# One core, eight stages: two PSUM banks shared by turns in the local layers, and the MLP norm's mean and variance in column quarters

## The chip, the cores and the metric

The program runs on 1 core of one Trainium2 chip. The time is the device time of one execution in microseconds, the median of three runs. The trace is of one further execution, taken by the hardware profiler. PE is TensorE, PEld its weight loads, DVE is VectorE, ACT is ScalarE, POOL is GpSimd, SP is SyncE, which here only issues DMAs.

## The reference

A stack of eight stages works on x of 16 sequences x 256 tokens x 128 channels, all in float32. The first seven (a random-feature attention, a router feed-forward, a cosine attention, an int4 linear layer, a state-space layer, an expert feed-forward, a gated recurrence) are touched only at the start and in the state-space layer. The last one, the local transformer, holds half the time:

```python
def attn_layer(x, Wqkv, qs, ksc, Wo):
    q, k, v = ...                      # 16 heads of 64
    q = l2norm(q) * qs ; k = l2norm(k) * ksc
    q = q * cos * scale + rotate_half(q) * sin * scale
    k = k * cos * inv + rotate_half(k) * sin * inv
    return local_attention(q, k, v) @ Wo        # window of 32
def ffn_layer(x, g, bln, W1, b1, W2, b2):
    mu = x.mean(-1, keepdims=True)
    var = ((x - mu) ** 2).mean(-1, keepdims=True)
    xn = (x - mu) / jnp.sqrt(var + 1e-05) * g + bln
    a, gate = jnp.split(xn @ W1 + b1, 2, -1)
    return a * jax.nn.gelu(gate, approximate=False) @ W2 + b2
for i in range(6):
    x = attn_layer(shift_tokens(x), ...) + x
    x = ffn_layer(shift_tokens(x), ...) + x
x = x + that_stack(_layernorm(x))
```

The state-space layer runs h = exp(delta A) h + delta x B over 256 tokens for 256 channels and 16 states, with an output projection.

## The kernel before

It is one program without a planner. Each stage is a block in which every engine has its own instruction stream, written out as a loop over steps; the streams are tied by semaphores, and each engine runs its stream in order. So the order of the work is the order of the calls in each engine's loop.

**Local layers** (`local_layers`). Tokens stand in 8 groups of 512 (two sequences), channels on the partitions (tile `y`). A step i takes one group and one quad of heads (four heads): 4 steps are a group, 32 a layer, N = 192 steps make the 6 layers. Work on different steps overlaps: step i projects queries and keys of quad i, norms those of i-1, scores i-2, takes values of i-2 and i-3. In this text a step has two halves:

- first half on PE: `project(4i)` (L2254, one 128x512 matmul), `project_v(2i)` (L2267), `norm(i-1)` (L2274), `score` of the even sequence (L2289), `project(4i+1)`, `values` of an odd sequence (L2309 for the values, L2313 for the sums that give the denominators);
- second half: `project(4i+2)`, `project_v(2i+1)`, `score` of the odd sequence, `project(4i+3)`, `values` of an even sequence.

The MLP of a group and the output projection lie between these calls, at fixed places by step modulo 4 (`mlp_at(i, k)`). I call the steps by what they carry: i mod 4 = 2 is the **out step** (L2324, output projection in two parts, the third gate matmul and gelu), 3 the **widen step** (three L2341), 0 the **back step** (L2363 in the first half; `center_mlp` L2332 and `variance` L2337 in the second), 1 the **gate step** (`make_gate` 0 and 1, L2341, in the second half; POOL's `scale_mlp` L2657 and ACT's `make_z` L2470 before them).

PSUM has 8 banks. All four projections of queries and keys go through bank 0, so `project(c)` waits for `squared` of c-1: DVE has multiplied the bank by the rotary tables (`rotate_start`, L2539 and L2540), and ACT has squared it (`square`, L2433). Bank 1 carries the values' projection, copied out by ACT (`copy_v`, L2449), and by turns the denominators, read by ACT (`take_den`, L2425 and L2427). Banks 2 to 5 are scores, 6 the values, and bank 7 (`X_BANK`) everything else: the norm's sums, output projection, mean, variance, gates, MLP; `take_x` makes each user wait until the one before has been read out.

The chain of a step's norm: `square` on ACT, `sum_squares` on POOL (L2645), `norm` on PE in the next step, `clamp` on DVE, `invert_norm` on ACT, four DMAs by SP that spread 32 rows to 128 (`send_inverse`), and `unite` on POOL (L2653), then the scores.

ACT's order in a first half: copy_v, square(4i), invert_norm, exp (L2455), square(4i+1), take_den, make_z. In a second: copy_v, square(4i+2), exp, take_gate (L2477), square(4i+3), take_den.

The MLP norm: PE multiplies `y` by the 128x128 matrix I - 1/128 (`center`), DVE copies the result to SBUF (L2577), ACT squares it, PE multiplies it by a 128x128 matrix of ones, so the variance stands on all 128 rows, and ACT takes Ln and Exp of 128x512.

**Prologue of the local layers**: DVE takes the statistics of all 32 tiles, and the 8 groups are normalized, transposed and copied one after another before the first step. **Start of the program**: SP issues the DMAs of x, nine constants and the weights of six stages, and only then do the engines begin. **State-space layer** (`state_space`): 16 steps (states) for each of 8 groups; the next group's statistics and transposes (MEASURE, NORMALIZE, TURN, TURNED) lie in steps 0 to 3, where the former group's gating, output projection (step 3, 12 small matmuls in one go) and addition (step 4) lie too.

## Time and profile before

| | |
|---|---|
| median of 3 runs | 6519.71 us (6516.19 to 6521.88) |
| profiled execution | 6522.74 us, span 6520.8 us |
| local layers, from first to last record | 3201.5 to 6518.1 us |
| granted TensorE clock, mean | 0.947 |

PE is busy for 90% of the span by its records, DVE for 67%, ACT 52%, POOL 35%. A record of a matmul is longer than the time in which the next one can start, so this text measures PE by the distance of the starts of neighbouring groups, not by their lengths. In the timeline a row is a group of equal neighbours: start, length, engine, line, operation, operands, count, and in brackets the idle time ahead of it and what ended it.

### The profile page before, as it was taken

To read this page: it belongs to the slowest core of one execution; us is meant where nothing else is said; L and a number is where in the kernel's file an instruction comes from. 1 tells how busy PE (TensorE), PEld (TensorE's weight loads), DVE (VectorE), ACT (ScalarE), POOL (GpSimd) and SP (SyncE) were. 2 spreads that over 40 slices of the span, in tenths; PEclk is the share of its full clock that TensorE was granted. 3 is DMA by queue.
4 is the path that set the end of the run, shared out by engine and by line. 5 is a ranking of instruction groups with operands and counts; after the bars stand their busy time and mean duration, and the time that the engine had idled before them with its cause. 6 is when DMAs were issued, how large, how long until landed. Compare 5 with 4: busy or idle time off the path is not lost.

```text
span 6520.8 us, 129965 instructions
## 1 busy us (share of the span) xinstructions
PE 5878.9 (90%) x51681; PEld 3219.8 (49%) x51681; DVE 4384.8 (67%) x7178; ACT 3402.6 (52%) x5560; POOL 2289.2 (35%) x1597
## 2 busy tenths in 40 slices
PE   7999878999677778998689999999999999999998
PEld 3555554444422225765445555555555555555554
DVE  4656434454288894334678888888878788887885
ACT  3444324656144443444456656666666666665664
POOL 0111101222034441000055555555555555555553
PEclk9999978999688888998799999999999999999998
DMA  5555302333100000000011111111111111111110
GB/s 138 115 115 119 89 0 53 80 82 83 44 3 0 0 0 1 1 0 1 24 36 32 40 43 34 31 47 37 34 45 38 33 44 40 34 39 41 38 37 24
DMA packets 298945, 275.95 MB, mean 42 GB/s; under 512 B 40580, under 2 KB 289572, under 8 KB 298148
## 3 DMA queue, kind: packets, MB, share of 16 engines
q1 hardware_dynamic: 298372, 268.00, 17.7%
q8 instruction: 397, 6.50, 0.4%
q14 instruction: 176, 1.44, 0.1%
HBM read 30.88 MB, written 2.10 MB: 5 GB/s over the span
## 4 chain that ended last, share of the span: by engine, by line
PE 33%; issue 5%; DVE 5%; POOL 5%; ACT 2%; DMA 0%; POOLq 0%; DVEq 0%; SPq 0%; ACTq 0%
PE banks L2254 7%; PE banks L2289 6%; PE banks L2324 5%; PE banks L2309 4%; PE banks L2267 3%; PE banks L2341 3%; DVE local_probs L2559 2%; POOL local_rot L2653 2%; POOL local_ssum L2645 2%; PE banks L2363 2%; PE banks L2313 2%; PE banks L2274 1%; ACT local_probs L2455 1%; DVE local_gate L2584 1%; DVE local_sin L2540 1%
## 5 line engine op out<-in xcount | busy, mean ns | idle before, releaser
L2645 POOL TENSOR_TENSOR local_ssum<-local_sq 128x512 f32<-128x512 f32 x384 | 697.5, 1816 | 2145.1 <-ACT local_sq L2433 2144.6
L2653 POOL TENSOR_TENSOR local_rot<-local_rot,local_inv_all 128x512 f32<-128x512 f32 x768 | 964.6, 1288 | 94.1 <-DMA local_inv_all<-local_inv 93.6
L2254 PE MATMUL banks<-local_y,local_Wqkv 128*128 128x512 f32 x1536 | 823.0, 618 | 64.0 <-ACT local_sq L2433 61.2
L2559 DVE TENSOR_TENSOR local_probs<-banks,band 128x576 f32<-128x576 f32 x768 | 546.2, 753 | 185.4 <-PE banks L2289 180.1
L2455 ACT ACTIVATE local_probs<-local_probs,local_npeak 128x1152 f32<-128x1152 f32 x384 | 482.8, 1257 | 357.1 <-DVE local_probs L2559 357.1
L2539 DVE TENSOR_TENSOR local_rot<-banks,local_rotary_scaled 128x512 f32<-128x512 f32 x768 | 525.6, 684 | 191.1 <-PE banks L2254 185.6
L2433 ACT ACTIVATE local_sq<-banks 128x512 f32<-128x512 f32 x768 | 459.4, 598 | 253.6 <-DVE local_sin L2540 244.8
L2546 DVE TENSOR_TENSOR local_rot<-local_rot,local_sin 128x1024 f32<-128x1024 f32 x384 | 513.7, 1338 | 41.9 <-DVE local_sin L2540 2.3
L2449 ACT COPY local_v<-banks 128x512 f32<-128x512 f32 x384 | 224.9, 586 | 594.1 <-PE banks L2267 593.6
L2289 PEld LDWEIGHTS banks<-local_rot 32*128 32x128 f32 x12288 | 416.7, 186 | 225.0 <-issue 200.8
L2540 DVE TENSOR_TENSOR local_sin<-banks,local_rotary_scaled 128x512 f32<-128x512 f32 x768 | 522.4, 680 | 0.0
L2309 PEld LDWEIGHTS banks<-local_probs,local_v 128*32 128x32 f32 x12288 | 345.4, 110 | 301.8 <-issue 291.9
L2289 PE MATMUL banks<-local_rot 32*128 32x160 f32 (+1 forms) x12288 | 490.2, 296 | 0.0
L1361 POOL TENSOR_TENSOR mamba_seen<-mamba_state,mamba_c_wide 128x1024 f32<-128x1024 f32 x128 | 301.0, 2352 | 474.2 <-DVE mamba_state L1442 474.2
L2309 PE MATMUL banks<-local_probs,local_v 128*32 128x160 f32 (+1 forms) x12288 | 458.5, 290 | 0.5 <-DVE local_oT L2567 0.5
L2254 PEld LDWEIGHTS banks<-local_y,local_Wqkv 128*128 128x128 f32 x1536 | 264.3, 190 | 372.1 <-ACT local_sq L2433 249.5
L1031 POOL TENSOR_TENSOR cosine_summed<-cosine_probs 128x512 f32<-128x512 f32 x128 | 162.4, 1269 | 696.1 <-ACT cosine_probs L919 696.1
L2267 PE MATMUL banks<-local_Wqkv,local_y 128*128 128x512 f32 x768 | 396.0, 597 | 0.0
L2324 PE MATMUL banks<-local_oT,local_Wo 128*128 128x512 f32 x768 | 354.9, 605 | 0.9 <-ACT local_gate L2477 0.9
L1258 PE MATMUL banks<-mamba_seen,ident 128*128 128x512 f32 x512 | 289.2, 693 | 64.8 <-DVE mamba_xs L1449 42.3
L2341 PE MATMUL banks<-local_mlp_z,local_W 128*128 128x512 f32 (+1 forms) x576 | 328.2, 652 | 11.9 <-DVE local_gate L2584 4.2
L487 POOL TENSOR_TENSOR favor_summed<-favor_probs 128x256 f32<-128x256 f32 x128 | 93.0, 727 | 689.3 <-DVE favor_probs L443 689.3
(400 smaller groups left out, 10561.4 us busy)
## 6 DMA issues: line engine op xcount, KB each, us to landing
local_inv_all<-local_inv SPq DMA_DIRECT2D x768, 128.0 KB, 2.7
favor_half_norm_all<-favor_half_norm SPq DMA_DIRECT2D x512, 128.0 KB, 3.0
cosine_inv_all<-cosine_inv SPq DMA_DIRECT2D x256, 128.0 KB, 2.6
favor_rden<-favor_inv SPq DMA_DIRECT2D x256, 64.0 KB, 2.1
cosine_rden<-cosine_inv_den SPq DMA_DIRECT2D x256, 64.0 KB, 2.1
local_Wqkv<-in_L_ffn_Wqkv_quads SPq DMA_DIRECT2D x36, 256.0 KB, 2.9
local_Wo<-in_L_ffn_Wo_quads SPq DMA_DIRECT2D x6, 512.0 KB, 4.1
experts_w_W<-in_L_ffn_W SPq DMA_DIRECT2D x1, 2048.0 KB
```

The costliest lines, as they stand in the source:

```text
L2254: pe.matmul(seqs(banks[:, QK_BANK, :]), Wqkv[:, at:at + P], y_group(g), start=True, stop=True).then_inc(qk_projected, 1)
L2267: pe.matmul(banks[:, V_BANK, :], y[:, 2 * g + tile // ST, at:at + P], Wqkv[:, V_COLUMNS(half)], start=True, stop=True).then_inc(v_projecte ...
L2289: last = pe.matmul(banks[:, S_BANK + r, lo:hi], k[rows_r, half, at:at + P], q[rows_r, half, at:at + hi - lo], start=(half == 0), stop=(hal ...
L2309: last = pe.matmul(banks[rows_r, O_BANK, part * SEQ + at:part * SEQ + to], v[:, G % 2, s * ST + tile, c:c + 32], probs[:, e % 3, r, lo:hi] ...
L2324: last = pe.matmul(banks[:, X_BANK, :], Wo[:, j, :], oT[:, (QUADS * G + j // 2) % (QUADS + 1), j % 2, :], start=(j == 0), stop=(j == 2 * Q ...
L2341: pe.matmul(banks[0:m, X_BANK, :], W1[:, column + lo:column + lo + m], z[:], start=True, stop=True).then_inc(signal, 1)
L2455: act.activation(a, a, ACT.Exp, bias=npeak[:, layer:layer + 1], scale=SCALE).then_inc(exped, 1)
L2539: dve.tensor_tensor(seqs(rot[:, k % ROTATED, half, :]), raw, twice(table[:, m, 0, half, :]), ALU.mult).then_inc(cosined, 1)
L2540: dve.tensor_tensor(seqs(sin[:, m, half, :]), raw, twice(table[:, m, 1, half, :]), ALU.mult).then_inc(sined, 1)
L2559: dve.tensor_tensor(probs[:, e % 3, r:r + 2, :], banks[:, S_BANK + r:S_BANK + r + 2, 0:SCORES], consts["band"].unsqueeze(1).broadcast_to([ ...
L2645: pool.tensor_tensor(ssum[:, n % 2, m, :], sq[:, 0, :], sq[:, 1, :], ALU.add).then_inc(square_summed, 1)
L2653: pool.tensor_tensor(a, a, twice(inv_all[:, n % 2, m, of_seq(s)]), ALU.mult).then_inc(united, 1)
```

## The change

It replaces several things at once.

1. **Local layers, banks.** Bank 0 now carries the even halves of queries and keys and the denominators, bank 1 the odd halves and the values' projection. `values` makes the denominators first, in bank 0, with a signal of its own (`den_summed`); ACT's `take_den` is cut in two, `log_den` (reads the bank) ahead of `exp` in ACT's order, and `invert_den` where take_den stood.
2. **Local layers, MLP norm.** The mean is four 128x32 by 128x128 matmuls (`mean`, in the widen step), read by ACT into `token_stat` (128x128), spread by four DMAs to 128x512; POOL subtracts (`center_mlp`, last in its step). The variance is made the same way, in the second half of the back step ahead of `project(4i+3)`; ACT's `root` works on 128x128 and stands ahead of `square(4i+3)`; four DMAs spread it; `scale_mlp` on POOL now stands behind `sum_squares(2i)`. DVE's copy goes.
3. **Local layers, prologue.** Only group 0 is prepared ahead; groups 1 to 7 in steps 0 to 7. The rotary tables of a layer are scaled in two parts around the layer's first step.
4. **State-space layer.** MEASURE to TURNED move to steps 12 to 15 of the former group, the output projection is cut in halves over steps 3 and 4, the addition goes to step 5.
5. **Start.** Only four constants, the first stage's weights and x are issued ahead; the other 43 DMAs go into SP's stream of the first stage, in its steps 1 to 6.

```diff
@@ start
-                for n in consts:
+                for n in FAVOR_CONSTS:
...
-                for name in ("router", "cosine", "int4", "mamba", "hgrn"):
-                    ws[name].load(sp)
@@ favor_attention, sync
+                    if i == LOADS:
+                        for tile, source in w["later_consts"]:
+                            sp.dma_start(tile, source).then_inc(w["consts_loaded"][0], 16)
+                    if 0 < i - LOADS <= len(w["later"]):
+                        w["later"][i - LOADS - 1].load(sp)
@@ state_space
-        0, 1, 2, 3, 5, 7, 8, 9, 10, 11, 12, 13, 14
-    GATE, WAY_OUT, ADD_OUT = 2, 3, 4
+        -4, -3, -2, -1, 5, 7, 8, 9, 10, 11, 12, 13, 14
+    GATE, WAY_OUT, ADD_OUT = 2, (3, 4), 5
@@ local_layers
-    QK_BANK, V_BANK, S_BANK, O_BANK, X_BANK = 0, 1, 2, 6, 7
+    DEN_BANK, V_BANK, S_BANK, O_BANK, X_BANK = 0, 1, 2, 6, 7
+    qk_bank = lambda c: (DEN_BANK, V_BANK)[c % 2]
@@ tensor, project
-                    if c:
-                        pe.wait_ge(squared, c)
+                    if half:
+                        pe.wait_ge(v_copied, c // 2 + 1)
+                    elif n >= 3:
+                        pe.wait_ge(den_logged, 2 * n - 5 + m)
+                    elif c:
+                        pe.wait_ge(squared, c - 1)
@@ project_v
-                    if j >= 6:
-                        pe.wait_ge(den_logged, j - 5)
-                    elif j:
-                        pe.wait_ge(v_copied, j)
+                    if j:
+                        pe.wait_ge(squared, 2 * j)
@@ values
+                    at_step = n + 2 + s
                     pe.wait_ge(exped, e + 1)
+                    if at_step < N:
+                        pe.wait_ge(squared, 4 * at_step + 3 - 2 * s)
+                    elif e:
+                        pe.wait_ge(den_logged, e)
+                    for lo, hi, tile in ((0, BAND, 0), (BAND, SCORES, 1)):
+                        for r in range(4):
+                            at = tile * P
+                            last = pe.matmul(banks[32 * r:32 * r + 32, DEN_BANK, at:at + hi - lo], consts["ones"][:, 0:32],
+                                             probs[:, e % 3, r, lo:hi], start=(tile == 0), stop=(tile == 1), skip_group_check=True)
+                    last.then_inc(den_summed, 1)
@@ mean, variance
-                    pe.matmul(seqs(banks[:, X_BANK, :]), center[:], y_group(G % GROUPS), start=True, stop=True).then_inc(centering, 1)
+                    for c in range(GT):
+                        at = c % ST * P
+                        last = pe.matmul(banks[32 * c:32 * c + 32, X_BANK, 0:P], consts["ones"][:, 0:32],
+                                         y[:, 2 * (G % GROUPS) + c // ST, at:at + P], start=True, stop=True)
...
-                    pe.matmul(banks[:, X_BANK, :], consts["ones"], msq[:], start=True, stop=True).then_inc(var_summed, 1)
+                    for c in range(GT):
+                        last = pe.matmul(banks[32 * c:32 * c + 32, X_BANK, 0:P], consts["ones"][:, 0:32], msq[:, c * P:(c + 1) * P],
+                                         start=True, stop=True)
@@ tensor, the order
+                    if (G := mlp_at(i, 7)) is not None:
+                        mean(G)
                     if i < N:
                         project(4 * i + 1)
...
                     if (G := mlp_at(i, 8)) is not None:
-                        center_mlp(G)
+                        variance(G)
...
-                    if (G := mlp_at(i, 8)) is not None:
-                        variance(G)
@@ scalar, the order
                         invert_norm(i - 1)
+                    if (e := within(2 * (i - 3) + 1)) is not None:
+                        log_den(e)
                     if (e := within(2 * (i - 2))) is not None:
                         exp(e)
+                    if (G := mlp_at(i, 7)) is not None:
+                        take_mean(G)
+                    if (G := mlp_at(i, 8)) is not None:
+                        square_mlp(G)
                     if i < N:
                         square(4 * i + 1)
                     if (e := within(2 * (i - 3) + 1)) is not None:
-                        take_den(e)
+                        invert_den(e)
...
+                    if (e := within(2 * (i - 2))) is not None:
+                        log_den(e)
                     if (e := within(2 * (i - 2) + 1)) is not None:
                         exp(e)
...
                     if (G := mlp_at(i, 8)) is not None:
-                        square_mlp(G)
+                        root(G)
                     if (G := mlp_at(i, 9)) is not None:
                         take_gate(G, 0)
                     if i < N:
                         square(4 * i + 3)
                     if (e := within(2 * (i - 2))) is not None:
-                        take_den(e)
-                    if (G := mlp_at(i, 8)) is not None:
-                        root(G)
+                        invert_den(e)
@@ gpsimd, the order
+                    if i < N:
+                        sum_squares(2 * i)
                     if (G := mlp_at(i, 9)) is not None:
                         scale_mlp(G)
-                    if i < N:
-                        sum_squares(2 * i)
...
                         sum_squares(2 * i + 1)
+                    if (G := mlp_at(i, 7)) is not None:
+                        center_mlp(G)
@@ sync
+                def send_token_stat(into, sent):
+                    for c in range(GT):
+                        rows_c = token_stat[32 * c:32 * c + 32, :]
+                        source = bass.AP(rows_c.tensor, rows_c.offset, [rows_c.ap[0], [0, 4], rows_c.ap[-1]])
+                        sp.dma_start(into[:, c * P:(c + 1) * P], source).then_inc(sent, 16)
```

## Rows read from the trace of the kernel before

**Rows 1.** The page, busy time of each engine
```profile
PE 5878.9 (90%) x51681; PEld 3219.8 (49%) x51681; DVE 4384.8 (67%) x7178; ACT 3402.6 (52%) x5560; POOL 2289.2 (35%) x1597
```

**Rows 2.** Timeline, first output-projection matmuls of two neighbouring groups
```profile
5006.01 3.70 PE L2324 MATMUL banks<-local_oT,local_Wo 128*128 128x512 f32 x8
...
5071.77 3.70 PE L2324 MATMUL banks<-local_oT,local_Wo 128*128 128x512 f32 x8
```

**Rows 3.** Timeline of PE in one gate step, and the next step's start
```profile
5052.61 0.67 PE L2313 MATMUL banks<-local_probs,ones 128*32 128x160 f32 x16
5053.99 1.12 PE L2254 MATMUL banks<-local_y,local_Wqkv 128*128 128x512 f32 x2 [0.71 <-ACT local_sq L2433]
5054.95 1.02 PE L2267 MATMUL banks<-local_Wqkv,local_y 128*128 128x512 f32 x2
5055.90 1.27 PE L2289 MATMUL banks<-local_rot 32*128 32x160 f32 x32
...
5058.06 1.02 PE L2254 MATMUL banks<-local_y,local_Wqkv 128*128 128x512 f32 x2
5059.02 1.19 PE L2309 MATMUL banks<-local_probs,local_v 128*32 128x160 f32 x32
5060.02 0.67 PE L2313 MATMUL banks<-local_probs,ones 128*32 128x160 f32 x16
5060.62 1.13 PE L2341 MATMUL banks<-local_mlp_z,local_W 128*128 128x512 f32 x2
...
5062.44 1.02 PE L2267 MATMUL banks<-local_Wqkv,local_y 128*128 128x512 f32 x2
5063.40 0.64 PE L2274 MATMUL banks<-local_ssum,local_heads 128*32 128x256 f32 x8
```

**Rows 4.** Timeline of ACT in that step
```profile
5054.66 0.80 ACT L2470 ACTIVATE local_mlp_z<-local_mlp_yc,local_ln_b,local_ln_g 128x512 f32<-128x512 f32 x1
...
5058.70 1.26 ACT L2455 ACTIVATE local_probs<-local_probs,local_npeak 128x1152 f32<-128x1152 f32 x1 [1.40 <-DVE local_probs L2559]
5059.86 0.67 ACT L2477 ACTIVATE local_gate<-banks,local_b 128x512 f32<-128x512 f32 x1
5060.45 0.60 ACT L2433 ACTIVATE local_sq<-banks 128x512 f32<-128x512 f32 x1
5060.94 0.38 ACT L2425 ACTIVATE local_rden<-banks 128x256 f32<-128x256 f32 x1
```

**Rows 5.** Timeline of POOL: that step's sum of squares, a later scaling of the MLP
```profile
5061.12 1.80 POOL L2645 TENSOR_TENSOR local_ssum<-local_sq 128x512 f32<-128x512 f32 x1 [0.41 <-ACT local_sq L2433]
...
5114.36 1.27 POOL L2657 TENSOR_TENSOR local_mlp_yc<-local_mlp_yc,local_mlp_sq 128x512 f32<-128x512 f32 x1 [0.30 <-ACT local_mlp_sq L2465]
```

**Rows 6.** Timeline of PE in a back step: the centering matmul and its follower
```profile
5108.24 1.13 PE L2332 MATMUL banks<-local_y,local_center 128*128 128x512 f32 x2
5109.20 1.02 PE L2254 MATMUL banks<-local_y,local_Wqkv 128*128 128x512 f32 x2
```

**Rows 7.** Busy time by stretches: us, each engine (instructions), granted clock, DMA share, GB/s
```profile
3236.00:3290.00 54.00, 38.21 (x209) 15.24 (x210) 31.69 (x51) 17.07 (x30) 20.84 (x14) 0.73 0.09 20
3290.00:3350.00 60.00, 52.94 (x694) 29.37 (x693) 47.58 (x66) 31.56 (x52) 35.24 (x24) 1.00 0.16 37
```

**Rows 8.** Timeline of the start: issue of x's rest, its use by DVE
```profile
9.12 1.14 SPq L2860 DMA_DIRECT2D x<-in_L_attn_x  x1
...
41.27 0.86 DVE L402 BATCH_NORM_STATS2 favor_stats<-x 128x6 f32<-128x128 f32 x4
```

**Rows 9.** DMA view of 0 to 80 us: KB each, median us to landing
```profile
x<-in_L_attn_x SPq DMA_DIRECT2D x1, 0.5 KB, 13.3
```

**Rows 10.** Timeline of the state-space layer: DVE behind the output projection
```profile
2090.88 1.23 DVE L1432 TENSOR_TENSOR banks<-mamba_dx,banks 128x1024 f32<-128x1024 f32 x1 [2.68 <-PE banks L1247]
```

**Rows 11.** Timeline of the local prologue: SP's last load, first table scaling
```profile
3213.79 0.37 SPq L2160 DMA_DIRECT2D local_W<-in_L_ffn_W  x1
...
3236.59 0.35 DVE L2527 TENSOR_SCALAR local_rotary_scaled<-local_rotary,local_qk_scales 128x256 f32<-128x256 f32 x1 [0.32 <-PEq L2168]
```

More of the change, by code:

```diff
@@ L1274, in _ @@
                         gather(k - 2)
-                    if (g := finish_at(k, WAY_OUT)) is not None:
-                        project_out(g)
+                    for half in range(2):
+                        if (g := finish_at(k, WAY_OUT[half])) is not None:
+                            project_out(g, half)
                     if (m := make_at(k, TURN)) is not None:
@@ L2216, in _ @@
                 act.preload_act_table_set(EXP_LN)
-                act.wait_ge(var_done, 1)
-                act.activation(ln_log, ln_var, ACT.Ln).then_inc(log_done, 1)
-                act.wait_ge(log_done, 1)
-                act.activation(ln_rstd, ln_log, ACT.Exp, scale=-0.5).then_inc(rstd_ready, 1)
-                for g in range(GROUPS):
-                    act.wait_ge(turned, g + 1)
-                    act.copy(y[low, 2 * g:2 * g + 2, 0:SEQ], seqs(banks[low, g, :])).then_inc(y_low, 1)
+                root_x(act, 0)
+                copy_x(act, 0)
             @block.tensor
             def _(pe):
-                for g in range(GROUPS):
-                    pe.wait_ge(normed, (g + 1) * GT)
-                    for tile in range(GT):
-                        last = pe.transpose(banks[:, g, tile * P:(tile + 1) * P], xn[:, g * GT + tile, :], consts["ident"])
-                    last.then_inc(turned, 1)
+                turn_x(pe, 0)
         with nc.Block() as block:
@@ L2432, in square @@
                         act.wait_ge(square_summed, c // 2)
[L2433 removed]
+                    act.activation(sq[:, c % 2, :], banks[:, qk_bank(c), :], ACT.Square).then_inc(squared, 1)
                 def invert_norm(n):
```

208 lines of the change are left out of this document (137 added, 71 removed).

## Prediction

> **What bounds the kernel now.** I read the page first: PE is busy for 90% of the span, DVE for 67% [rows 1]. Half of the time is the local layers, so I took a period of them, one group in four steps: from one output projection to the next 65.76 us [rows 2]. Then the timeline of PE through the four steps, reading only starts. In the gate step one group of matmuls follows the other at a fixed distance (for instance 0.96, 0.95, 0.96, 1.00, 0.60) but for one place: the sums of L2313 start at 5052.61, and the next projection not 0.60 but 1.38 us behind them, and the bracket names ACT's square as releaser [rows 3]. That 0.78 us is the only stall that I find in the period, so PE has 65.0 us of work in 65.8. DVE, in a stretch of the same loop, is busy for 48 of 60 us where PE has 53 [rows 7]. So the local layers are bound by PE. PE's stream is in order: what is taken from its work is gained, and a wait that is put into it counts in full, since nothing later can be pulled ahead of it.
>
> **PE's work.** The centering matmul takes 0.96 us to its follower [rows 6], and the variance has the same shape. Each becomes four 128x32 matmuls over 128 columns. The nearest rows are the norm's four over 256 columns, 0.64, and the eight of the denominators, 0.60 for 1152 columns [rows 3]; half of the first is 0.32, 512 of 1152 columns of the second are 0.27. I take 0.35 (bounds 0.25 and 0.64). So 1.92 becomes 0.70: a gain of 1.22 us per group. The denominators only change places with the values. The 0.78 us of today's wait goes too, and what is late next is counted now.
>
> **The waits.** I count from T, the start of a half step's odd projection (`project(4i+1)` or `project(4i+3)`). By today's distances, PE's stream behind it, with nothing of the MLP between, is: denominators at 1.05 (1.00 for the projection by its rows, up to 0.05 more where no MLP matmul stood ahead), the rest of `values` to 2.65, the even projection (5060.62 to 5062.44, less 0.96 for the gate matmul) to 3.5, the values' projection (0.96) to 4.46, where in the second half the norm follows [rows 3].
> On ACT `log_den` now stands ahead of `exp`. It waits for the denominators: 1.05 + 0.67 [rows 3] + 0.07 for the signal (from square's end to POOL's start in rows 4 and 5) = T+1.79, and takes 0.38 [rows 4]. So `exp` starts at T+2.20, where today it starts as soon as the mask is done, and frees ACT 1.16 later [rows 4]: T+3.36. `square` takes 0.60 [rows 4]: T+3.96. POOL's sum takes 1.75 to 1.80 [rows 5], so the norm can start at T+5.85. Since the odd projection now sits in bank 1, the values' projection waits for that same square: T+4.02. Put against PE's stream:
> - gate step, first half: the values' projection wants T+3.50, gets T+4.02: 0.52 us.
> - gate step, then: `scale_mlp` now stands behind `sum_squares(2i)` on POOL: 3.96 + 0.07 + 1.76 + 1.27 [rows 5] = 7.06, `make_z` 0.80 [rows 4], signals: 7.95. PE wants the first gate matmul at 4.02 + 0.95 + 1.20 (scores: 5055.90 to 5058.06 less the gate matmul) = 6.17. Wait 1.8 us. Today `make_z` is done at 5055.46, before the scores have even begun [rows 3, 4].
> - gate step, second half: the second gate matmul needs bank 7 emptied by `take_gate` (0.67, rows 4), which is behind `exp`: T+4.08, wanted at T+2.65: 1.43 us. The norm is then no longer late.
> - widen step, first half: the same with `take_mean` (128x128; between half and the whole of the 0.38 in rows 4, I take 0.28): the first L2341 gets T+3.69, wants T+2.65: 1.04 us.
> - widen step, second half: one L2341 lies between, the norm wants T+5.41, gets T+5.85: 0.44 us.
> - back step, second half: the variance that filled 0.96 us here has moved ahead, and `root` (Ln and Exp of 128x128, 0.45 to 0.9, I take 0.66) stands between `exp` and `square`. Square ends at T+4.62. The values' projection waits 1.16, and the norm, at T+6.50, another 0.88: 2.04 us.
> - out step: the output projection and the third gate matmul cover all of it: 0.
> The spreads of mean and variance are covered: POOL uses the mean at the end of that step, the variance a step later; SP's four issues each stand behind those of `send_inverse`, and nobody waits for what comes behind them. POOL's new subtraction (bounds 1.27 and 1.80, rows 5) is last in its step, ahead of a wait for the next squares.
> Sum of waits 7.27 us. The period becomes 65.76 - 0.78 - 1.22 + 7.27 = 71.03, +5.27. DVE loses a copy and stays below PE. For 46 of the 48 groups (the first and the last are not in the pattern): +242 us. Bounds: with the 0.4 and 0.5 terms gone and half of the gate step's, +3 a group, +140; with 0.2 us more at each of seven waits, +6.7, +308.
>
> **The rest.** Start: DVE gets to the second group at 41.27, long after x's rest has landed at 9.12 + 13.3 = 22.4 us [rows 8, 9]. With five constants fewer ahead and nothing behind, it lands at 18 to 20 (estimate), so the start gains 21 to 23. Against it 43 DMAs of 0.4 to 1.1 us of issue [rows 8, 11], some 25 us of SP's time, go between the first stage's own transfers, where SP has gaps: I charge 5 (0 to 20). Net -17 (-24 to 0). State-space layer: DVE waits 2.68 us per group behind the output projection [rows 10]; halving it gains at most that, for 8 groups -20 (-30 to 0; it would cost if the statistics, now in steps 12 to 15, delayed DVE there). Local prologue: the tables are scaled from 3236.6, and SP's loads end at 3214.2 [rows 11], which now becomes the limit: -22, of which the preparation of groups 1 to 7 in the early steps gives some 7 back: -15 (-22 to -3). Scaling the tables, eight of at most 0.35 us [rows 11] at each layer's start, now lies largely beside PE's work: -7 (-11 to 0). Together -59 (-87 to -3).
>
> Sum: +242 - 59 = +183 on the profiled execution of 6522.7, so 6706; the median lies 3 us lower: **6703**.
>
> **The rivals.**
> Waits that vanish (other side). If PE had slack that I overlook, or `exp` did not have to wait for `log_den`, only the work counts: 65.76 - 0.78 - 1.22, -2.0 a group, -96, and -59: 6365 us. For it speaks that two banks now share eight fillings by turns, where one had four that each waited for DVE and ACT. Against it: this wait is 0.78 us of 65.8 today, and the places of the calls fix mine. It decides from where the waits sum to under 3.3 us per group. Chance 0.12.
> Waits of half my size, 3.7 us, if they overlap with each other more than I count: about 6535. Chance 0.11 (0.04 of it faster, 0.05 the same, 0.02 slower).
> A lower clock. In 3236 to 3290, with PE busy for 38 of 54 us, the granted clock was 0.73; in the next stretch, 53 of 60 us, it was 1.00 [rows 7], the higher of its two levels (2.4 GHz). With my waits PE is busy for about 90% of a period, so I expect 1.00. Should 4 us of matmuls in each group run at 1.2 GHz, they take 4 us more, +190: 6890. Chance 0.08. The Trainium skill (TensorE: Matmul & The Clock Gate, section A second HAM failure mode: psum-queue depth-cycling) says that a kernel that cycles through PSUM banks can idle so often for moments that the clock swings between its levels; by that rule this rival would be the likely one. The stretch with 53 of 60 us speaks against it.
> That the change doesn't do what it says: the early loads may slow the first stage by all that the start gains. It costs 20 us and is in the range.
>
> **How the numbers follow.** My forecast has 0.69, the others 0.12, 0.11, 0.08. Faster by over 0.2% (13 us, about what a measurement of this kernel tells from no change): 0.12 + 0.04 = 0.16. Same 0.05. Slower 0.69 + 0.08 + 0.02 = 0.79. The range: the low bounds, +140 - 87 = +53, are widened to the half-sized waits: 6510; the high ones, +308 - 3 = +305, give 6825, of which I take 6810, since not all come together. Outside lie the vanished waits, the fast part of the half-sized ones and half of the lower clock, 0.2.
>
> **What would show it.** In the local layers of the changed kernel: 71 us between output projections; 1.8 us of idle PE ahead of the first gate matmul with `make_z` as releaser, 1.4 ahead of the second with ACT's gate copy; 1.0 ahead of the first widening matmul with `take_mean`; 2 us in two parts ahead of the norm behind the back step; ACT's `exp` starting 2.2 us behind the odd projection in every half. The clock stays 1.00. The state-space layer is 20 us shorter and the first stage ends 17 us earlier. If the period is under 65.8 us, my reading of ACT's order is wrong.

## The result, and the profile after

The changed kernel takes 6596.2 us (median of four runs, 6595.5 to 6598.6) where the kernel before takes 6518.0 on the same chip (6512.9 to 6521.9): ratio 1.0119, interval 1.0104 to 1.0134. It is 78 us slower; the forecast was 183 us slower, 6703 us. The sign and the places of the waits were right, the size was not. The profiled executions lie 74.3 us apart (spans 6520.8 and 6595.1).

From the page of the changed kernel, busy time of each engine [against rows 1]:

```profile
PE 5843.6 (89%) x52257; PEld 3191.9 (48%) x52257; DVE 4346.5 (66%) x7129; ACT 3319.8 (50%) x5630; POOL 2137.8 (32%) x1645
```

PE has 35 us less to do, and the span is 74 us longer: the time is in PE's waits. By the first and last record of each layer the 74 us split so: the first layer ends 18.8 us earlier, the state-space layer is 8.9 us shorter (696.3 to 687.5), the local layers need 18.3 us less from their first record to their first output projection (138.1 to 119.8), and 117.9 us more from the first to the 48th (3120.7 to 3238.6). The rest adds 2.4 us, in pieces of under 2.

Two neighbouring output projections in the timeline of PE [against rows 2]:

```profile
5024.49 3.70 PE L2358 MATMUL banks<-local_oT,local_Wo 128*128 128x512 f32 x8
...
5093.75 3.70 PE L2358 MATMUL banks<-local_oT,local_Wo 128*128 128x512 f32 x8
```

The period is 69.26 us, and nearly all 47 are within 0.05 of it. In the kernel before they were not alike: 65.75 to 66.1 in most periods of the middle layers, up to 67.4 in the others, 68 to 70.7 at the five boundaries between layers. Without the last period, which is cut short in both, the mean is 66.63 before and 69.22 after.

The gate step of the changed kernel on PE, with idle time and releaser in brackets [against rows 3]. L2285 projects, L2334 is the denominators, L2346 the values, L2296 the values' projection, L2318 the scores, L2382 the gate matmuls:

```profile
5001.15 1.12 PE L2285 MATMUL banks<-local_y,local_Wqkv 128*128 128x512 f32 x2
5002.20 0.70 PE L2334 MATMUL banks<-local_probs,ones 128*32 128x160 f32 x16
5002.72 1.16 PE L2346 MATMUL banks<-local_probs,local_v 128*32 128x160 f32 x32
5003.81 1.12 PE L2285 MATMUL banks<-local_y,local_Wqkv 128*128 128x512 f32 x2
5005.03 1.12 PE L2296 MATMUL banks<-local_Wqkv,local_y 128*128 128x512 f32 x2
5006.09 1.27 PE L2318 MATMUL banks<-local_rot 32*128 32x160 f32 x32
5008.54 1.10 PE L2382 MATMUL banks<-local_mlp_z,local_W 128*128 128x512 f32 x2 [1.18 <-issue]
5009.47 1.02 PE L2285 MATMUL banks<-local_y,local_Wqkv 128*128 128x512 f32 x2
...
5013.35 1.13 PE L2382 MATMUL banks<-local_mlp_z,local_W 128*128 128x512 f32 x2 [1.24 <-ACT local_gate L2530]
```

ACT and POOL in the same stretch [against rows 4, 5]. L2469 is `log_den`, L2501 `exp`, L2479 `square`, L2523 `make_z`, L2530 `take_gate`, L2711 the sum of squares, L2727 `scale_mlp`:

```profile
5002.97 0.38 ACT L2469 ACTIVATE local_rden<-banks 128x256 f32<-128x256 f32 x1 [1.15 <-PE banks L2334]
5003.25 1.25 ACT L2501 ACTIVATE local_probs<-local_probs,local_npeak 128x1152 f32<-128x1152 f32 x1
5004.40 0.59 ACT L2479 ACTIVATE local_sq<-banks 128x512 f32<-128x512 f32 x1
...
5007.63 0.81 ACT L2523 ACTIVATE local_mlp_z<-local_mlp_yc,local_ln_b,local_ln_g 128x512 f32<-128x512 f32 x1 [2.25 <-POOL local_mlp_yc L2727]
...
5011.47 1.25 ACT L2501 ACTIVATE local_probs<-local_probs,local_npeak 128x1152 f32<-128x1152 f32 x1
5012.62 0.68 ACT L2530 ACTIVATE local_gate<-banks,local_b 128x512 f32<-128x512 f32 x1
```

```profile
5005.06 1.30 POOL L2711 TENSOR_TENSOR local_ssum<-local_sq 128x512 f32<-128x512 f32 x1 [5.73 <-ACT local_sq L2479]
5006.32 1.27 POOL L2727 TENSOR_TENSOR local_mlp_yc<-local_mlp_yc,local_mlp_sq 128x512 f32<-128x512 f32 x1
```

The chain for the first gate matmul is read downwards: square to 5004.99, sum to 5006.36, scaling to 5007.59, `make_z` to 5008.44, matmul at 5008.54. The bracket of that matmul names no releaser ("issue"); in 39 of 45 groups the list below names `make_z`. The second stands behind `log_den`, `exp` and `take_gate`. The other waits of a group that have a bracket, in the widen and the back step (L2507 is `take_mean`, L2644 is `hide`, DVE's step of the MLP that multiplies the widened part by its gate):

```profile
5041.63 1.12 PE L2382 MATMUL banks<-local_mlp_z,local_W 128*128 128x512 f32 x2 [0.83 <-ACT local_token_stat L2507]
...
5052.27 0.64 PE L2303 MATMUL banks<-local_ssum,local_heads 128*32 128x256 f32 x8 [0.34 <-DVE local_gate L2644]
...
5067.23 1.13 PE L2296 MATMUL banks<-local_Wqkv,local_y 128*128 128x512 f32 x2 [0.69 <-ACT local_sq L2479]
5068.59 0.64 PE L2303 MATMUL banks<-local_ssum,local_heads 128*32 128x256 f32 x8 [0.23 <-POOL local_ssum L2711]
```

The view that should have been read first is the list of PE's waits over all the local layers, 3300 to 6400 us (what waited, for whom: us in total, times, longest). Before:

```profile
PE banks L2254 <- ACT local_sq L2433: 45.1, 58, 2.1
PE banks L2274 <- DVE local_gate L2584: 17.2, 28, 0.9
PE banks L2274 <- POOL local_ssum L2645: 13.1, 20, 1.9
```

After:

```profile
PE banks L2382 <- ACT local_gate L2530: 56.0, 45, 1.2
PE banks L2382 <- ACT local_mlp_z L2523: 47.6, 39, 1.2
PE banks L2382 <- ACT local_token_stat L2507: 36.7, 44, 0.8
PE banks L2296 <- ACT local_sq L2479: 32.7, 47, 0.8
PE banks L2303 <- DVE local_gate L2644: 15.8, 44, 0.7
PE banks L2303 <- POOL local_ssum L2711: 10.8, 46, 1.0
PE banks L2382 <- issue: 7.1, 6, 1.2
```

In sum 75 us of waits before, 207 after. Before there were three kinds of them, not one: besides the 0.71 to 0.78 in every group, PE waited in some groups for DVE's `hide(G, 2)` and for POOL's sum ahead of the norm.

### The profile page after: what moved, and what is told of

Read it like the earlier page. It is cut to its first block and busy times, and to the rows that moved or that the text cites. A ratio compares the mean times of both kernels' runs of the same rounds, so it can differ in the third digit from the quotient of the medians.

```text
span 6595.1 us, 132318 instructions
## 1 busy us (share of the span) xinstructions
PE 5843.6 (89%) x52257; PEld 3191.9 (48%) x52257; DVE 4346.5 (66%) x7129; ACT 3319.8 (50%) x5630; POOL 2137.8 (32%) x1645
## 5 line engine op out<-in xcount | busy, mean ns | idle before, releaser
L2711 POOL TENSOR_TENSOR local_ssum<-local_sq 128x512 f32<-128x512 f32 x384 | 498.9, 1299 | 2445.0 <-ACT local_sq L2479 2437.7
L2719 POOL TENSOR_TENSOR local_rot<-local_rot,local_inv_all 128x512 f32<-128x512 f32 x768 | 958.9, 1282 | 61.6 <-DMA local_inv_all<-local_inv 61.1
L2285 PE MATMUL banks<-local_y,local_Wqkv 128*128 128x512 f32 x1536 | 821.8, 617 | 12.3 <-PEq L2215 8.0
L2479 ACT ACTIVATE local_sq<-banks 128x512 f32<-128x512 f32 x768 | 455.8, 594 | 158.8 <-DVE local_sin L2603 156.9
L2609 DVE TENSOR_TENSOR local_rot<-local_rot,local_sin 128x1024 f32<-128x1024 f32 x384 | 498.3, 1298 | 41.9 <-DVE local_sin L2603 2.3
L2318 PEld LDWEIGHTS banks<-local_rot 32*128 32x128 f32 x12288 | 416.4, 186 | 225.0 <-issue 208.2
L2318 PE MATMUL banks<-local_rot 32*128 32x160 f32 (+1 forms) x12288 | 489.7, 296 | 0.5 <-POOL local_rot L2719 0.5
L2501 ACT ACTIVATE local_probs<-local_probs,local_npeak 128x1152 f32<-128x1152 f32 x384 | 478.6, 1246 | 3.7 <-DVE local_probs L2622 3.6
L2382 PE MATMUL banks<-local_mlp_z,local_W 128*128 128x512 f32 (+1 forms) x576 | 328.1, 652 | 168.0 <-ACT local_gate L2530 59.9
L2346 PE MATMUL banks<-local_probs,local_v 128*32 128x160 f32 (+1 forms) x12288 | 448.0, 286 | 0.3 <-DVE local_oT L2631 0.3
L2296 PE MATMUL banks<-local_Wqkv,local_y 128*128 128x512 f32 x768 | 403.5, 607 | 44.4 <-ACT local_sq L2479 39.9
L2469 ACT ACTIVATE local_rden<-banks 128x256 f32<-128x256 f32 x384 | 147.6, 384 | 585.9 <-PE banks L2334 585.6
L2631 DVE TENSOR_TENSOR local_oT<-banks,local_rden 128x512 f32<-128x512 f32 x384 | 265.3, 691 | 221.6 <-ACT local_rden L2473 213.0
L2285 PEld LDWEIGHTS banks<-local_y,local_Wqkv 128*128 128x128 f32 x1536 | 263.6, 189 | 276.4 <-issue 227.5
L2346 PEld LDWEIGHTS banks<-local_probs,local_v 128*32 128x32 f32 x12288 | 376.5, 110 | 9.5 <-issue 0.5
```

The source lines that it names most:

```text
L2285: pe.matmul(seqs(banks[:, qk_bank(c), :]), Wqkv[:, at:at + P], y_group(g), start=True, stop=True).then_inc(qk_projected, 1)
L2296: pe.matmul(banks[:, V_BANK, :], y[:, 2 * g + tile // ST, at:at + P], Wqkv[:, V_COLUMNS(half)], start=True, stop=True).then_inc(v_projecte ...
L2318: last = pe.matmul(banks[:, S_BANK + r, lo:hi], k[rows_r, half, at:at + P], q[rows_r, half, at:at + hi - lo], start=(half == 0), stop=(hal ...
L2346: last = pe.matmul(banks[rows_r, O_BANK, part * SEQ + at:part * SEQ + to], v[:, G % 2, s * ST + tile, c:c + 32], probs[:, e % 3, r, lo:hi] ...
L2479: act.activation(sq[:, c % 2, :], banks[:, qk_bank(c), :], ACT.Square).then_inc(squared, 1)
L2501: act.activation(a, a, ACT.Exp, bias=npeak[:, layer:layer + 1], scale=SCALE).then_inc(exped, 1)
```

## The experiments

The theory: what is slow is the order of the steps on ACT and POOL. `log_den` waits for the denominators until T+1.8 (T: start of the odd projection of a half step) and holds `exp` back; the small steps that empty bank 7 (`take_mean`, `root`, `take_gate`) stand behind both; `scale_mlp` stands behind the sum of squares. The main rival: the two shared banks, or the MLP norm by transfers, cost the time themselves, and a wait taken away comes back at the next shared bank. "A mean period" below leaves out the cut last one of 47; it is 66.63 before and 69.22 changed. Times are medians of four to eleven executions, but for three runs with one (named there). The cuts of code show the calls alone, without the conditions around them.

**Order, one engine at a time.** POOL alone (e1):

```diff
-                    if i < N: sum_squares(2 * i)
                     if (G := mlp_at(i, 9)) is not None: scale_mlp(G)
+                    if i < N: sum_squares(2 * i)
```

> POOL only: scale_mlp goes back ahead of sum_squares(2i), as in the kernel before. Theory (order of steps on ACT and POOL makes the waits): make_z then ends at about T+5 of the gate step, the first gate matmul's wait of 1.25 us goes, the other waits stay (0.36, 1.32, 0.91, 0.41, 0.96, 0.41). 1.25 x 46 = 57: 6539 us, period 67.97. Rival (the two shared banks or the transfers themselves cost the time, and a wait that is taken away comes back at the next shared bank): the wait moves to the gate step's second half, 6585 to 6600 us.

Measured 6536.7 us, mean period 68.03 (-1.19). The 47.6 us of waits for `make_z` are gone; 56.0 for the gate copy, 37.5 for `take_mean` and 33.4 for the square stand as they were, within 1 us. The wait did not come back.

ACT alone, the small steps (e2):

```diff
-    log_den(2(i-3)+1); exp(2(i-2)); take_mean(G)
+    take_mean(G); log_den(2(i-3)+1); exp(2(i-2))
...
-    log_den(2(i-2)); exp(2(i-2)+1); root(G); take_gate(G, 0)
+    root(G); take_gate(G, 0); log_den(2(i-2)); exp(2(i-2)+1)
```

> ACT only: take_mean, root and take_gate(G, 0), the three that empty bank 7, go ahead of log_den, which waits for the denominators until T+1.8 anyway. Theory: the second gate matmul's wait of 1.32 and the first widening matmul's 0.91 go, the values' projection of the back step waits 0.36 instead of 0.96: 2.83 x 46 = 130: 6466 us, period 66.4. Rival (shared banks): ACT's exp and square do not move, so PE is held one step later by the square, and no more than 1 us a group is gained: 6550 or more.

Measured 6475.4 us, mean period 66.76 (-2.46): the theory's terms (2.83) within a sixth, and 75 us below the rival's bound.

ACT alone, the two long ones (e3):

```diff
-    log_den(2(i-3)+1); exp(2(i-2))
+    exp(2(i-2)); log_den(2(i-3)+1)
...
-    log_den(2(i-2)); exp(2(i-2)+1)
+    exp(2(i-2)+1); log_den(2(i-2))
```

> ACT only: exp goes ahead of log_den in both halves, as in the kernel before; the small steps stay behind both. Theory: in the second halves of gate and back step the mask is long done and exp starts 1.5 to 2.7 us earlier, so gate1's wait falls from 1.32 to 0.2 and the back step's 0.96 and 0.41 vanish; in the first halves exp starts only 0.5 earlier, log_den ends at T+3.1, and the even projection of the gate step, which now needs the denominators' bank, waits 0.45 that it did not wait: together -2.65 a group, 6474 us. Rival (log_den must stand first because the banks are shared): the even projections of all four steps wait 0.5 each: -0.5 a group, 6570.

Measured 6478.6 us, mean period 66.79 (-2.43). PE's waits in the local layers, two of them:

```profile
PE banks L2285 <- ACT local_rden L2469: 18.9, 43, 0.5
PE banks L2382 <- ACT local_token_stat L2507: 11.5, 46, 0.3
```

The first is new: the even projection now waits for `log_den`, once a group, 0.44 us, since the denominators share its bank. This is all that `log_den` ahead of `exp` protects: 0.44 us in one half step of eight, where `log_den` behind `exp` gains 2.9 in the others.

POOL's order and ACT's small steps together (e4, the edits of e1 and e2):

> The edits of e1 and e2 together. Theory: the terms add, since they lie at different places of the group: 1.25 + 2.83 = 4.08 us, 188 in all: 6408 us, period 65.1, faster than the kernel before. Rival: they overlap, because the shorter gate step leaves the mask and exp later against the odd projection: 6440 or more.

Measured 6439.6 us, mean period 66.10: 1.2% faster than the kernel before (ratio 0.9878, 0.9861 to 0.9894), but 32 us short of the sum of the terms, which is the rival's number (6440 or more). The rival put it down to a later `exp`; the list of waits names POOL and, with 18.7 us, `hide(G, 2)`, and POOL's timeline shows it (L2719 is `unite`, four in a row):

```profile
PE banks L2303 <- POOL local_ssum L2711: 36.7, 76, 1.9
```

```profile
5059.94 5.96 POOL L2719 TENSOR_TENSOR local_rot<-local_rot,local_inv_all 128x512 f32<-128x512 f32 x4 [0.92 <-DMA local_inv_all<-local_inv]
5065.86 1.27 POOL L2711 TENSOR_TENSOR local_ssum<-local_sq 128x512 f32<-128x512 f32 x1
```

In the gate step the second sum of squares stands behind four unites, which start only when the transfer of the inverse norms has landed. With a shorter gate step PE gets to the norm before POOL gets to the sum.

**Exp where its mask is ready.** In the second halves of the back and the gate step `exp` went ahead of `log_den` as well (e5: `root`, `take_gate`, `exp`, `log_den`):

> The edits of e4, and in the second halves of the back and the gate step exp goes ahead of log_den too (behind root or take_gate), since the mask is done there before log_den's wait ends. Theory: the back step's square ends at T+3.4 instead of 3.84, so its two waits (0.36 for the values' projection, 0.36 for the norm, 0.04 and 0.29 beyond the bare distance) shrink by 0.5 to 0.7, and the gate step's norm wait (0.44 idle, POOL's unites start late) by 0.1 to 0.4, since that norm chain starts earlier: -0.6 to -1.1 a group, 6390 to 6410 us. Rival (POOL's chain of unites is what binds now): only the back step's 0.3 goes, 6425.

Measured 6425.0 us, mean period 65.59: the rival's number. What PE still waited for was POOL's sum, 29.4 us, and DVE's `hide(G, 2)`, 18.3 us.

**POOL's and DVE's order too (e10).**

```diff
-    unite x4; sum_squares(2 * i + 1)
+    unite x2 (first sequence); sum_squares(2 * i + 1); unite x2 (second)
...
-    normalize(2(i-2)); hide(G, 2)
+    hide(G, 2); normalize(2(i-2))
```

> The edits of e5, and two more changes of order: on POOL sum_squares(2i+1) goes between the unites of the two sequences (the second pair is needed a half step later), on DVE hide(G, 2) goes ahead of normalize, which waits for invert_den. Theory: the gate step's norm no longer waits for POOL's four unites (mean 0.41 a group beyond the bare 0.95), the widen step's norm no longer for hide(G, 2) (0.41 to 0.55): -0.8 a group, 6387 us, period 64.5. Rival (the scores of the next step then wait for the later unites, or DVE's normalize comes late): the gain is under 0.3 a group, 6411 or more.

Measured 6382.7 us (6381.6 to 6386.7), ratio 0.9796 (0.9781 to 0.9811): 2.0% faster than the kernel before, 3.2% faster than the changed one. Nearly every period away from a boundary is 64.48 or 64.49; in e5 they ran from 64.9 to 66.5. PE's two longest waits in the local layers are

```profile
PE banks L2303 <- POOL local_ssum L2714: 11.0, 48, 1.5
PE banks L2382 <- DVE local_gate L2647: 5.4, 5, 2.5
```

**Which part of the change costs.** The changed kernel with the old MLP norm (e6), and the kernel before with the new one (e7); each change of code is the hunks for `center_mlp`, `mean`, `variance`, `take_mean`, `root`, `take_centered`, `scale_mlp`, `send_mean` and `send_rstd`, backward or forward.

> The changed kernel with the MLP norm of the kernel before (centering matmul, DVE copy, full-width variance behind the values, root behind the denominators, scale_mlp ahead of the sum of squares); the two shared banks stay. Theory, against 6596: +1.20 us of PE work a group; waits -1.25 (scale), -0.91 (take_mean), -0.85 (variance covers the back step's norm again); the gate copy's 1.32 stays: -1.8 a group, 6512 us, period 67.1. Rival A (the shared banks are the cost): 6590 or more. Rival B (the banks are free, the new norm is the whole cost): period at 65.0 to 65.7, 6430 to 6460.

> The kernel before with the new MLP norm alone (mean and variance on 32 rows by quarters, spread by transfers, in the places of the change); one bank for the projections and ACT's order of exp ahead of the denominators stay. Theory, against 6516: PE work -1.20 a group; new waits 0.85 (scale behind the sum), 0.45 (mean's copy behind exp), 1.05 (root ahead of square in the back step, where the variance no longer covers it): +1.15, 6570 us. Rival (the norm is a pure gain, the two banks make the waits): -1.20 a group, 6460.

Measured 6561.4 and 6547.4 us, mean periods 68.57 and 67.26: +1.94 and +0.63 against 66.63, together +2.57, where the whole change has +2.59. (e6 also holds the change's new places of the tables and of the prologue.) So the parts add up, and neither of the rivals "the one is free" holds: as placed, the banks cost three times what the norm does. Both forecasts were off, by 49 us upward and 23 downward. With the banks alone PE waits

```profile
PE banks L2371 <- ACT local_mlp_sq L2498: 57.4, 45, 1.3
PE banks L2375 <- ACT local_gate L2516: 56.0, 45, 1.2
```

The first line I had not foreseen: with the old norm `square_mlp` too stands behind `log_den` and `exp`, and the variance matmul waits 1.28 us for it. It is the same mechanism once more. With the norm alone

```profile
PE banks L2254 <- ACT local_sq L2440: 86.5, 146, 3.1
PE banks L2348 <- ACT local_mlp_z L2484: 31.7, 39, 0.8
```

the scaling behind the sum costs 0.81 to 0.88 a group as counted (0.85), `root` ahead of the square 0.60 instead of my 1.05, and the mean's copy 0.05 instead of 0.45. A fourth wait was not in my sum: in the back step the odd projection stands 0.73 us behind the variance that now takes 0.36, since the square is not done, which is 0.37 more (the 146 waits of the first line are three a group). With it the terms give 0.65 a group (1.85 of waits less 1.20 of work), and 0.63 was measured.

**The kernel before, with orders alone.** POOL's order (e13), then POOL's, DVE's and ACT's (e14):

> The kernel before with POOL's order of e10 alone: sum_squares(2i+1) between the unites of the two sequences. Theory (the periods of the kernel before lie between 65.75 and 67.1 because that sum stands behind four unites and their transfer): PE's 13.1 us of waits for POOL's sum go, and the periods away from a layer's boundary become equal: -13 us, 6503. Rival (the spread of the periods has another source, or the sum is then still late): 6510 to 6516.

Measured 6504.3 us (ratio 0.9978, 0.9969 to 0.9987), the theory's number. Nearly every period away from a boundary is 65.75 now, so it was POOL's order that spread them. The boundary periods are longer than they were (72.2 to 72.7), which takes back 16 of 27 us: the longest wait for the square is 3.9 us there, where it was 2.1. What makes it longer was not tried.

> The kernel before with three changes of order alone: POOL's of e13, hide(G, 2) ahead of normalize as in e10, and take_gate(G, 0) ahead of exp. Banks, MLP norm, tables and start as before. Theory (the 75 us that PE waits in the kernel before, 1.6 a group and not 0.78, are of order): the waits for the square (45.1, of which about 11 belong to the layers' boundaries), for hide(G, 2) (17.2) and for POOL (13.1) go but for the boundaries: -64 us, 6452. So two thirds of what separates e10 (6383) from the kernel before need neither the shared banks nor the transfers. Rival (the one bank for the projections binds: the square's wait stays whatever stands ahead of it): 6485 or more.

Measured 6498.1 us (0.9967, 0.9955 to 0.9979), period 65.63. Here my theory fell (6452) and the rival's number held. PE's list of waits has one line:

```profile
PE banks L2254 <- ACT local_sq L2433: 55.1, 58, 4.1
```

The 0.71 us wait of each group stands in the first half of the gate step, where no gate copy is in the way. The rows of one such place, where the projection that fills the bank starts at 5039.26 and PE's work behind it is done at 5041.92 (L2559 is the mask, L2539 and L2540 the two products of the bank):

```profile
5039.40 1.42 DVE L2559 TENSOR_TENSOR local_probs<-banks,band 128x576 f32<-128x576 f32 x2 [0.78 <-PE banks L2289]
5040.74 0.68 DVE L2539 TENSOR_TENSOR local_rot<-banks,local_rotary_scaled 128x512 f32<-128x512 f32 x1
5040.86 1.26 ACT L2455 ACTIVATE local_probs<-local_probs,local_npeak 128x1152 f32<-128x1152 f32 x1 [1.24 <-DVE local_probs L2559]
5042.05 0.60 ACT L2433 ACTIVATE local_sq<-banks 128x512 f32<-128x512 f32 x1
5042.70 1.13 PE L2254 MATMUL banks<-local_y,local_Wqkv 128*128 128x512 f32 x2 [0.71 <-ACT local_sq L2433]
```

The bank's own round (projection, two products on DVE, square on ACT) is part of it, but not all: DVE starts the products behind its mask, 0.4 us after the projection's follower has started on PE (5040.32), and the square also stands behind `exp`. My estimate from these rows is that the round alone would leave some 0.4 of the 0.78 us. Whether DVE's products ahead of the mask and ACT's square ahead of `exp` would take the rest away in the kernel before was not tried. In the runs with the shared banks this wait is gone. So the orders that I tried are worth 19 us in the kernel before; the whole change with good orders 132.

**The small parts.** The scaled tables alone, in the kernel before (e12):

> The kernel before with the new places of the scaled rotary tables alone. Read are the five periods that hold a layer's boundary: 68.70, 69.80, 67.95, 68.39, 70.67 us before, beside neighbours of 65.8 to 67. Theory (the tables' eight steps on DVE make the boundary): each falls to within 1 us of its neighbours, -10 to -14 us in all. Rival (weights or another wait make it): under -4 us.

One execution, 6510.0 us, inside the spread of the kernel before beside it (6509.3 to 6519.8). The five boundary periods were 67.45, 67.45, 71.10, 71.50 and 68.21: three fell by 1.3 to 2.5, two rose by 3, and their sum did not fall at all (345.5 before, 345.7 here). So the theory (-10 to -14) fell, and the rival's number holds. The sum of the 47 periods fell by 5.7, all of it away from the boundaries, 2.3 in the cut last one. PE's list of waits shows why: those for the square fell from 45.1 to 36.7 us, their longest from 2.1 to 0.7, and a line is there that the kernel before does not have, once at each boundary, of nearly the same sum:

```profile
PE banks L2254 <- ACT local_sq L2433: 36.7, 56, 0.7
PE banks L2341 <- DVE local_gate L2584: 7.8, 5, 2.8
```

The second widening matmul waits for `hide(G, 0)`, and in the step ahead of a boundary the first tables are now scaled by DVE ahead of just that. e10 has the same five waits (5.4 us), and its boundary periods are together 18 us longer than their neighbours, as against 17 in the kernel before. Why two of them are 2.8 us long and three short I did not settle, nor was the place of the tables tried apart.

The state-space layer, read by its own length (695.2 to 696.4 in five runs of the old form; 684.9 to 689.3 in eight of the changed one, median 685.6). The changed kernel with the statistics and transposes back (e8):

```diff
-    MEASURE, NORMALIZE, TURN, TURNED ... = -4, -3, -2, -1
+    MEASURE, NORMALIZE, TURN, TURNED ... = 0, 1, 2, 3
```

> The changed kernel with the state-space layer's statistics and transposes back in steps 0 to 3; its output projection stays in two halves and its addition in step 5. Read is that stage's length: 696.3 us before, 687.5 changed. Theory (the halves bring little because the addition in step 5 now holds up the widening matmuls of the same step, whose drive wait grew from 1.58 to 3.05; the gain is that of the moved transposes): 697 to 701 us. Rival (the halves bring the gain, the moved transposes cost part of it): 675 to 685 us.

One execution, 692.8 us: between both theories' numbers; the halves alone gain 3. The changed kernel with the projection whole again (e9):

```diff
-    GATE, WAY_OUT, ADD_OUT = 2, (3, 4), 5
+    GATE, WAY_OUT, ADD_OUT = 2, (3, 3), 4
```

> The changed kernel with the state-space layer's output projection whole again, in step 3, its addition in step 4; statistics and transposes stay moved. Read is that stage's length: 696.3 before, 687.5 changed, 692.8 with the halves alone. Theory: the wait behind the projection is 2.7 again, the one behind the widening matmuls 1.6 again instead of 3.05, the others as in the changed kernel: 683 to 688 us. Rival (both parts are needed): 692 or more.

One execution, 688.5 us, half a us above the theory's range, and 688.6 in e11. The moved transposes alone bring 7.5 of the 10. What the halves add to them is not clear: 688.5 lies within the 684.9 to 689.3 of the changed form. DVE in the changed kernel shows where the wait went [against rows 10]:

```profile
2154.56 1.23 DVE L1442 TENSOR_TENSOR banks<-mamba_dx,banks 128x1024 f32<-128x1024 f32 x1 [1.02 <-PE banks L1256]
...
2165.84 1.23 DVE L1442 TENSOR_TENSOR banks<-mamba_dx,banks 128x1024 f32<-128x1024 f32 x1 [3.05 <-PE banks L1256]
```

The 2.68 us behind the projection become 1.02 and 0.57, and the 1.58 us two steps on become 3.05. With the projection whole that is 1.57 again. That the addition, now in the same step as the widening matmuls that reuse its bank, is the cause was argued from the order; it was not tried apart.

Everything together, with the loads later in the first layer and the projection whole (e11):

> The edits of e10, the loads of the later layers from step 8 of the first layer on instead of step 1, and the state-space layer's output projection whole in step 3 with its addition in step 4 (its statistics and transposes stay in the new steps 12 to 15). Theory: first layer 4 to 6 us shorter than the 783.0 of the changed kernel, since the eight transfers of a step are then not held up while PE is still short of work; state-space layer at 683 to 688 us (the halving brought nothing in the changed kernel, 687.5): 6375 to 6385 us. Rival (loads cost the same wherever they stand, halves are worth having): 6390 to 6400.

6388.2 us (0.9805, 0.9791 to 0.9818), between both forecasts and no better than 6382.7. The first layer takes 783.2 us, inside the 781.8 to 784.8 of the runs that load early, so the theory on the loads fell: they cost the same in the middle of the layer. PE's waits moved with them: the changed kernel has 1.90 us at 58.7 and 2.38 at 85.3, among its early loads, the kernel before has neither; here both are gone, and 4.91 us stand at 138.9, among the late loads.

## Why the prediction was right or wrong

The mechanism was right: ACT's and POOL's order puts waits into PE's stream. What failed is the size of the local layers' term: forecast +235 us (242 less 7 for the tables), measured +117.9. Two steps of the working make nearly all of these 117 us: the sum of waits of 7.27 us a group, of which 5.62 were measured (about 76 us), and the sentence that the 0.78 us are the only stall, from one quiet period (about 40 us).

**PE's work.** Right: the mean and the variance take 0.36 us each (forecast 0.35), and a group's work without waits is 69.25 - 5.62 = 63.63 us (forecast 63.76).

**The waits.** All seven stand where they were forecast, with the named releasers but one. Distance to the follower less its undisturbed distance (the first has no bracket in the trace, so there the releaser is by the order alone): gate step 0.36, 1.25, 1.32 (forecast 0.52, 1.8, 1.43); widen step 0.91, 0.41 (1.04, 0.44); back step 0.96, 0.41 (1.16, 0.88). Sum 5.62 where the forecast had 7.27. Two terms of the sum were mis-sized. The first is the cadence of ACT: `exp` begins 0.28 us behind `log_den`, the square 1.15 behind that, and ends at T+3.84, not 3.96; `take_mean` adds 0.15 and not 0.28. The second is POOL's sum of squares: 1.27 to 1.30 us and not 1.76, which took 0.5 us off the first gate matmul's wait and 0.3 to 0.5 off the norm's. The one releaser that was wrong is the widen step's norm: it waited for `hide(G, 2)` on DVE, behind `normalize`, and not for POOL; its size came out right by chance.

**The reference period.** This is the error in the reading of the old trace. I measured one period in a quiet layer, 65.76 us, and wrote that its stall was the only one. The mean before was 66.63, 40 us more over 46 periods: 17 of them lie in the five boundary periods, the rest mostly where PE waited for `hide(G, 2)` and for POOL's sum (30 us in the list). The longer waits of the changed kernel covered all of that: nearly all of its periods are equal. So 0.87 of the 2.68 us that separate +5.27 from +2.59 are this, 1.65 are the waits and 0.13 the work.

**The rivals.** Waits that vanish: false as placed, but e10 shows that the price was one of order and not of the banks; with `exp` still behind `log_den` in six halves of eight the period is 64.48. Half-sized waits was the nearest to the result by its number (its 6535 lay 61 us off, the forecast 107), not by its reason: the waits did not overlap, and they were 0.77 of mine, not half. Lower clock: false. The granted clock in 4900 to 5500, with waits of 1.2 us in each group:

```profile
4900.00:5500.00 600.00, 557.10 (x6680) 298.34 (x6679) 465.50 (x660) 342.47 (x589) 283.68 (x228) 1.00 0.19 45
```

PE is busy for 93%, at the higher level of the clock (1.00, 2.4 GHz). What the Trainium skill says of kernels that cycle through PSUM banks (TensorE: Matmul & The Clock Gate, section A second HAM failure mode: psum-queue depth-cycling) did not occur here.

**The start** went as counted. x's rest is used at 19.03, forecast to land at 18 to 20, and PE's values projection behind the first queries starts 25.1 us earlier (46.12 to 21.03); 6 of that are lost again by the layer's end (forecast 5), among the loads, as the waits that move with them show. Net -18.8, forecast -17.

```profile
19.03 0.87 DVE L409 BATCH_NORM_STATS2 favor_stats<-x 128x6 f32<-128x128 f32 x4 [6.86 <-DMA x<-in_L_attn_x]
```

**The local prologue** was forecast at -15 and measured -18.3: the first scaling of a table stands 12 us behind the stage's first record and not 35, which is 23 (forecast 22), and 5 are given back (forecast 7). **The state-space layer** was forecast at -20 and measured -8.9 (-10 by the median of all runs with the same code): I took a wait for gained that mostly moved two steps on. **The tables**, -7: no run shows it. Alone, their new place left the sum of the five boundary periods as it was (+0.2 us): what PE no longer waited for the square, it waited for `hide(G, 0)`.

## What to carry to other kernels

Before setting the cost of a change against a period, add up the waits of the bound engine over all periods, by releaser: one period read closely gave 0.78 us of stall where the mean had 1.6, and long new waits can hide small old ones, so that the difference is less than the sum. When banks or buffers are shared by turns, place the steps on the engine that frees them by who waits for whom: a step that waits itself goes behind those that are ready, and small steps that empty a bank go ahead of the long ones. The same edit then went from 1.2% slower to 2.0% faster, with no instruction added or removed.

## What the runs showed of the hardware

POOL's sum of squares takes 1.27 us alone, and longer, by most of the time that it spends beside DVE's `rotate_end`. In the kernel before:

```profile
5060.52 1.27 DVE L2546 TENSOR_TENSOR local_rot<-local_rot,local_sin 128x1024 f32<-128x1024 f32 x1
```

beside the sum of rows 5, which starts 0.67 us before that instruction ends and takes 1.80. Over 3400 to 6300 us of the kernel before, sums that share no time with a `rotate_end` have a mean of 1.27 us (7 of them), those that share 0.63 us in the mean 1.76 (280), those that share 1.04 us in the mean 2.17 (61); in the changed kernel 329 of 335 share under 0.25 us, mean 1.28. It holds the other way round: a `rotate_end` that starts while POOL is at work takes up to 2.3 us instead of 1.23. The Trainium skill has this (SBUF — State Buffer, sections SBUF: two separate sides, and Who interferes with whom): VectorE with two SBUF inputs and GpSimd share a pair of ports, whoever comes first has it for the whole instruction, and the other stands still. The traces agree with it within 0.2 us: 0.49 longer for 0.63 shared, 0.90 for 1.04. I had read 1.75 to 1.80 as the price of the instruction, when it was the price of its neighbour; the change moved the neighbour.

On ACT, independent instructions overlap by about 0.1 us (`exp` takes 1.25 us and its follower starts 1.15 behind it), and `exp` starts 0.28 us after the start of a `log_den` that takes 0.38. A chain worked out from durations is too long by 0.1 us a link; one from starts is not.
